# Token rows scattered to expert slots, results added in HBM, attention ahead of the routed experts

## The chip, the cores and the metric

One core of one Trainium2 chip runs the whole program. The metric is the device time of one execution in microseconds; the median of three runs stands for the kernel. A core has five engines that follow their own instruction streams and wait for one another by semaphores: PE (TensorE, matrix products, with its weight loads as PEld), DVE (VectorE), ACT (ScalarE), POOL (GpSimd) and SP (SyncE, which here only issues transfers). Indirect transfers, whose row numbers are data, are issued by POOL.

## The reference

2048 tokens of 128 numbers. With `xn` the layer norm of the input, the result is `x + attention(xn) + experts(xn)`.

```
xn = layernorm(x)
# attention, linear, 16 heads of 8
q, k, v = split(layer_norm(xn) @ Wqkv);  q, k = elu(q) + 1, elu(k) + 1
att = (q @ (k^T v)) / (q @ sum(k) + 1e-6)            # per head and batch
attention = xn + att @ Wout
# experts: 8, top 2, 640 slots each
top_v, top_i = top_k(xn @ Wg.T, 2);  gates = softmax(top_v)
pos  = running count of the expert's choices;  keep = pos < 640
h    = gelu(rows @ W1[:, :256]) * (rows @ W1[:, 256:]);  y = h @ W2
out[token] += gate * y[expert, slot]                 # for kept choices
```

## The kernel before

**Dense expert and routed experts.** Expert 0 is computed for all 2048 tokens in four groups of 512 and multiplied by a gate that is zero where it was not chosen. Experts 1 to 7 are routed: each has 640 slots, 5 tiles of 128 rows, computed as a step of 3 tiles and a step of 2 (`PARTS`). The first two dense groups run early, before attention's projections; the other two come last, after all routed steps (`DENSE_AFTER`). Products are made as three fp32r products of high and low halves (`product`, L973 to L975), so every input needs a split: the high half by ACT, the low half by a subtraction on POOL (`lower_w1`, L435, `xT_lo` L441) or DVE.

**Routing.** DVE takes the two best experts of each token (L749 to L760) from logits in a PSUM bank. PE counts the choices ahead of each (L1055, L1057), DVE turns the counts to slots (L772 to L784). Then a list of the token in each slot is made: DVE builds 0/1 matrices (`hot`, and `hot_row` of 128x4096 at L800), PE multiplies them (L1075, 32 matmuls), and DVE copies the list `slot_token` out (L817).

**Rows in and out.** `xn` is stored to HBM. POOL gathers the 35 tiles of 128 rows by 35 indirect transfers (`gather`, L459), five tiles per expert, and scatters the 35 result tiles by 35 indirect transfers (`scatter`, L471) into `y_rows`, which has one row per token and choice, zeroed before. Five experts' gathers are issued ahead of the first scatter (`GATHERS_AHEAD`), then the two take turns. In `y_rows` no two rows meet. At the end SP waits for all 35 scatters (L375), fetches both halves of `y_rows` in eight transfers (L378), DVE, ACT and POOL weight them by the gates and add them to the sum (L838, L663, L491), and SP stores the output (L385).

**Attention** is 14 pieces of work: four transposes of queries, and for eight pairs of tiles a numerator, a transpose and a projection. `ATT_FROM`, `ATT_EVERY` place them between the products of routed steps 9 to 14 and the dense ones after. The order of the work on each engine is written out by hand from these tables.

Of the kernel before, what the change touches and what calls it, by code (L numbers as in the profile page):

```python
# [5 lines left out]
F32 = mybir.dt.float32  # L20
# [17 lines left out]
DENSE_AFTER = (7, 7)  # L38
ATT_FROM = 36
ATT_EVERY = 2  # L40
ATT_DENSE = 14
GATHERS_AHEAD = 5
LO_EARLY = 2
EARLY_SUMS = 2
KV_LAG = 8
RESULTS_AT = 2
SLOTS_AT = 4
LIST_AT = 2
PRE_POOL = 2
DROPPED = 8192.0  # L50
PARTS = ((0, 3), (3, 2))


def moe_attention_block(nc, x, gamma, beta, wqkv, wout, wg_t, w1, w2, out):
# [15 lines left out]
    assert D == P and CAP % P == 0 and sum(n for _, n in PARTS) == ST and N <= 2048 and FC == 2  # L70

# [3 lines left out]
    steps = []  # L75
    for r, (e, j0, nj) in enumerate(routed_steps):
        steps.append((e, j0, nj, r))
        if (r + 1) % len(PARTS) == 0:
            steps += [step for step, after in zip(all_token_steps[EARLY:], DENSE_AFTER)
                      if after == (r + 1) // len(PARTS)]  # L80
    assert EARLY + len(steps) == len(routed_steps) + len(all_token_steps)
    S = len(steps)
    step_of_routed = [s for s in range(S) if steps[s][3] is not None]
    dense_steps = [s for s in range(S) if steps[s][3] is None]
    U = T // 2
    KT = TOP_K * T

# [7 lines left out]

    hurried = [s for s in range(1, S) if steps[s - 1][3] is not None and steps[s][3] is None][-1]
    spots = [(s, c, i) for s in range(S) for c in range(FC) for i in range(2)]
    chunks = [(s, c) for s in range(S) for c in range(FC)]
    pieces_at = {}
    i = ATT_FROM  # L100
    for piece in pieces:
        pieces_at.setdefault(spots[i] if i < len(spots) else "end", []).extend(piece)
        i += ATT_EVERY if i < 2 * FC * ATT_DENSE else 1

# [7 lines left out]
    for s, c in chunks:  # L112
        assert not pieces_at.get((s, c, 0)) or s >= EARLY_SUMS + EARLY
        if c == 0 and EARLY_SUMS <= s < EARLY_SUMS + EARLY:
            for j in range(GROUP):
                note_sum(("early", s - EARLY_SUMS), (all_token_steps[s - EARLY_SUMS][1] + j,))
        for kind, u in pieces_at.get((s, c, 0), []) + pieces_at.get((s, c, 1), []):
            if kind == "projection":
                note_sum((kind, u), (2 * u, 2 * u + 1))
        if s >= 1 and c == FC - 1 and steps[s - 1][3] is None:  # L120
            for j in range(GROUP):
                note_sum(("step", s - 1), (steps[s - 1][1] + j,))
    for kind, u in pieces_at.get("end", []):
        if kind == "projection":
            note_sum((kind, u), (2 * u, 2 * u + 1))
    assert steps[-1][1] == T - GROUP and steps[-1][3] is None
    for t in range(0, T, 2):
        if t == T - GROUP:
            for j in range(GROUP):
                note_sum(("step", S - 1), (t + j,))  # L130
        for k in range(TOP_K):
            note_sum(("fetched", t, k), (t,))
# [7 lines left out]
    xn_rows = nc.dram_tensor("xn_rows", [N, D], F32).ap()  # L140

    y_rows = nc.dram_tensor("y_rows", [TOP_K * N + R * CAP, D], F32).ap()
    xn_rows_tiles = xn_rows.rearrange("(t p) d -> p t d", p=P)
    y_rows_tiles = y_rows[0:TOP_K * N, :].rearrange("(t p) d -> p t d", p=P)

    with ExitStack() as ctx:
# [3 lines left out]
        def sem(name):  # L150
# [5 lines left out]
        xn = sb("xn", [P, T, D])  # L156
# [20 lines left out]
        iota_tiles = sb("iota_tiles", [P, RT, KT], F16)  # L177
        token_id = sb("token_id", [P, TOP_K, T], F16)
        first_slot = sb("first_slot", [P, T, E])
        rank = sb("rank", [P, T, E])  # L180
        eps = sb("eps", [P, 1])
        unused = sb("unused", [P, 1])
        unused_gelu = sb("unused_gelu", [P, 1])
# [10 lines left out]
        logit = sb("logit", [P, T, E])  # L194
# [4 lines left out]
        best = sb("best", [P, T])  # L199
# [3 lines left out]
        gate = [sb(f"gate{k}", [P, T]) for k in range(TOP_K)]  # L203
        gate_routed = [sb(f"gate_routed{k}", [P, T]) for k in range(TOP_K)]
        assigned = sb("assigned", [P, T, E], BF16)
        kept = sb("kept", [P, T, E])
# [5 lines left out]
        row_i = sb("row_i", [P, TOP_K, T], I32)  # L212
        tile_i = sb("tile_i", [P, TOP_K, T], I32)
        row_16 = sb("row_16", [P, TOP_K, T], F16)
        tile_16 = sb("tile_16", [P, TOP_K, T], F16)
        kept_routed = sb("kept_routed", [P, TOP_K, T])
        no_token = sb("no_token", [P, RT])
        vacant = sb("vacant", [P, RT])
        choices = sb("choices", [P, RT])
        target = sb("target", [P, RT])  # L220
        slot_target = sb("slot_target", [P, RT], I32)
        zeros = sb("zeros", [P, D])
        gate_dense = sb("gate_dense", [P, T, E])
        gate_part = sb("gate_part", [P, T, E])
        hot = sb("hot", [P, 2 * RT, KT], F16)
        hot_token, hot_tile = hot[:, 0:RT, :], hot[:, RT:2 * RT, :]
        slot_token = sb("slot_token", [P, RT], I32)

        gathered = sb("gathered", [P, RT, D])

        iota_rows = gathered[:, :, :].rearrange("p n d -> p (n d)")[:, 0:P * KT // 2] \
            .bitcast(F16).rearrange("p (r n) -> p r n", n=KT)
        xg_hi = [sb(f"xg_hi{i}", [P, 3 * P], F32R) for i in range(2)]
# [1007 lines left out]
```

## Time and profile before

| | |
|---|---|
| median of 3 runs | 187.8 us (181.33, 187.8, 189.93) |
| span of the profiled execution, first to last instruction | 156.1 us |
| median less span | 31.7 us |
| busiest engines | PE 111.6 us, POOL 99.3 us |

The profiled execution has only its span; its own device time is not given, so the difference to the median is what lies ahead of the first and behind the last instruction, together with the spread between runs. Busy shares are means over the span. A group of rows gives the idle time in front of its instructions and what ended it. The chain that ended last runs backwards from the last instruction through what released each wait; it tells which engine set the time in each stretch.

### The profile page before, as it was taken

To read this page: it belongs to the slowest core of one execution; us is meant where nothing else is said; L and a number is where in the kernel's file an instruction comes from. 1 tells how busy PE (TensorE), PEld (TensorE's weight loads), DVE (VectorE), ACT (ScalarE), POOL (GpSimd) and SP (SyncE) were. 2 spreads that over 40 slices of the span, in tenths; PEclk is the share of its full clock that TensorE was granted. 3 is DMA by queue.
4 is the path that set the end of the run, shared out by engine and by line. 5 is a ranking of instruction groups with operands and counts; after the bars stand their busy time and mean duration, and the time that the engine had idled before them with its cause. 6 is when DMAs were issued, how large, how long until landed. Compare 5 with 4: busy or idle time off the path is not lost.

```text
span 156.1 us, 2323 instructions
## 1 busy us (share of the span) xinstructions
PE 111.6 (72%) x745; PEld 103.8 (66%) x745; DVE 93.8 (60%) x251; ACT 72.2 (46%) x165; POOL 99.3 (64%) x111
## 2 busy tenths in 40 slices
PE   0029998399978996999999949609989999630000
PEld 0019975288978994999999949609989887620000
DVE  0699989999668838866535322504276565426940
ACT  0457669356659885054645535403243343124600
POOL 7950369934337777777777777777777777305540
PEclk9999999999999999599999999975899999996555
DMA  4999995000002222222121211121111111189540
GB/s 119 269 375 341 337 347 165 0 0 6 0 0 62 43 53 50 49 58 60 44 62 50 57 50 50 50 50 54 51 50 60 58 53 54 35 227 302 153 124 0
DMA packets 20827, 15.49 MB, mean 99 GB/s; under 512 B 2032, under 2 KB 18672, under 8 KB 20816
## 3 DMA queue, kind: packets, MB, share of 16 engines
q1 hardware_dynamic: 17856, 10.49, 22.7%
q0 software_dynamic: 2240, 4.59, 11.6%
q10 hardware_dynamic: 720, 0.27, 0.8%
q8 instruction: 6, 0.10, 0.3%
q14 instruction: 5, 0.04, 0.1%
HBM read 8.85 MB, written 6.49 MB: 98 GB/s over the span
## 4 chain that ended last, share of the span: by engine, by line
POOL 43%; DVE 16%; issue 15%; PE 11%; DMA 8%; ACT 2%; SPq 1%; DVEq 0%; POOLq 0%; ACTq 0%
POOL gathered L459 22%; POOL y_rows L471 21%; PE bank_y L993 4%; DVE xs L838 4%; DMA expo<-y_rows 4%; DMA xs<-in_x 3%; PE bank_a L1075 2%; PE bank_x L986 2%; DVE hid L765 2%; DMA y_rows<-gathered,slot_target 1%; DVE chosen L753 1%; PE bank_x L1046 1%; DVE stats L684 1%; DVE eq L751 1%; DVE xn L697 1%
## 5 line engine op out<-in xcount | busy, mean ns | idle before, releaser
L459 POOL DMA_INDIRECT gathered<-xn_rows,slot_token x35 | 34.3, 980 | 14.8 <-issue 10.4
L471 POOL DMA_INDIRECT y_rows<-gathered,slot_target x35 | 34.0, 972 | 10.7 <-issue 10.7
L940 DVE TENSOR_TENSOR hid<-gelu,bank_h 128x384 f32<-128x384 f32 (+2 forms) x32 | 16.4, 511 | 20.9 <-ACT gelu L645 20.5
L1197 PE MATMUL bank_y<-w_sb,hid 128*128 128x128 f32 x172 | 24.1, 293 | 1.3 <-issue 1.3
L1197 PEld LDWEIGHTS bank_y<-w_sb,hid 128*128 128x128 f32 x172 | 23.3, 210 | 1.5 <-issue 1.4
L645 ACT ACTIVATE gelu<-bank_h 128x384 f32<-128x384 f32 (+2 forms) x32 | 14.6, 458 | 19.8 <-PE bank_h L975 19.8
L973 PE MATMUL bank_h<-xg_hi,w_lo 128*128 128x384 f32 (+1 forms) x56 | 21.0, 375 | 1.3 <-DVE hid L940 0.9
L975 PE MATMUL bank_h<-xg_hi,w_hi 128*128 128x384 f32 (+1 forms) x56 | 17.8, 317 | 0.0
L974 PE MATMUL bank_h<-xg_lo,w_hi 128*128 128x384 f32 (+1 forms) x56 | 17.6, 315 | 0.0
L973 PEld LDWEIGHTS bank_h<-xg_hi,w_lo 128*128 128x128 f32 x56 | 11.1, 199 | 2.1 <-issue 1.3
L986 PE MATMUL bank_x<-ident,xn 128*128 128x128 f32 x16 | 4.4, 428 | 11.0 <-DVE xn L697 9.7
L491 POOL TENSOR_TENSOR xs<-xs,expo 128x256 f32<-128x256 f32 x8 | 6.1, 761 | 9.6 <-ACT expo L663 6.1
L1155 PE MATMUL bank_x<-ident,gathered 128*128 128x128 f32 x35 | 6.7, 292 | 7.6 <-DMA gathered<-xn_rows,slot_token 7.1
L628 ACT ACTIVATE gathered<-bank_y 128x384 f32<-128x384 f32 (+1 forms) x14 | 6.1, 438 | 12.5 <-PE bank_y L1197 12.5
L435 POOL TENSOR_TENSOR w_lo<-w_raw,w_hi 128x512 fp32r<-128x512 f32 x8 | 10.3, 1317 | 2.3 <-ACT w_hi L530 2.3
L913 DVE TENSOR_TENSOR xg_lo<-bank_x,xg_hi 128x384 fp32r<-128x384 f32 (+1 forms) x14 | 6.8, 488 | 8.1 <-ACT xg_hi L618 8.1
L838 DVE SCALAR_TENSOR_TENSOR xs<-expo,gate_routed,xs 128x128 f32<-128x128 f32 x16 | 8.0, 519 | 5.6 <-DMA expo<-y_rows 5.3
L974 PEld LDWEIGHTS bank_h<-xg_lo,w_hi 128*128 128x128 f32 x56 | 11.1, 198 | 0.0
L975 PEld LDWEIGHTS bank_h<-xg_hi,w_hi 128*128 128x128 f32 x56 | 11.0, 196 | 0.0
L986 PEld LDWEIGHTS bank_x<-ident,xn 128*128 128x128 f32 x16 | 3.2, 240 | 11.3 <-issue 9.6
L1155 PEld LDWEIGHTS bank_x<-ident,gathered 128*128 128x128 f32 x35 | 4.4, 147 | 8.8 <-DMA gathered<-xn_rows,slot_token 7.8
L618 ACT ACTIVATE xg_hi<-bank_x 128x384 fp32r<-128x384 f32 (+1 forms) x14 | 6.1, 436 | 8.3 <-PE bank_x L1155 8.3
(151 smaller groups left out, 266.8 us busy)
## 6 DMA issues: line engine op xcount, KB each, us to landing
w_raw<-in_w SPq DMA_DIRECT2D x4, 512.0 KB, 7.8
y_rows<-zeros SPq DMA_DIRECT2D x2, 1024.0 KB, 11.8
expo<-y_rows SPq DMA_DIRECT2D x8, 256.0 KB, 5.3
xs<-in_x SPq DMA_DIRECT2D x4, 256.0 KB, 4.6
xn_rows<-xn SPq DMA_DIRECT2D x4, 256.0 KB, 4.3
out_block<-xs SPq DMA_DIRECT2D x4, 256.0 KB, 2.3
w_sb<-in_w SPq DMA_DIRECT2D x1, 768.0 KB, 10.8
gathered<-xn_rows,slot_token POOLq DMA_INDIRECT x35, 2.7
```

What stands on the lines that cost most here:

```text
L435: nc.gpsimd.tensor_tensor(w1_lo[:, e, :], w1_raw[:, e, :], w1_hi[:, e, :].bitcast(F32), ALU.subtract).then_inc(w1_lo_ready, 1)
L459: nc.gpsimd.indirect_dma_start(gathered[:, n, :], None, xn_rows, bass.IndirectOffsetOnAxis(ap=slot_token[:, n:n + 1], axis=0),).then_inc(r ...
L471: nc.gpsimd.indirect_dma_start(y_rows, bass.IndirectOffsetOnAxis(ap=slot_target[:, n:n + 1], axis=0), gathered[:, n, :], None,).then_inc(y ...
L645: nc.scalar.activation(gelu[i % 2][:, 0:cols], bank_h[2 * c][:, 0:cols], ACT.Gelu).then_inc(gelu_ready, 1)
L838: nc.vector.scalar_tensor_tensor(acc[:, t, :], fetched[:, k, t, :], gate_routed[k][:, t:t + 1], acc[:, t, :], ALU.mult, ALU.add).then_inc( ...
L940: nc.vector.tensor_tensor(hid[s % 2][:, c, 0:cols], gelu[i % 2][:, 0:cols], bank_h[2 * c + 1][:, 0:cols], ALU.mult).then_inc(hid_ready, 1)
L973: nc.tensor.matmul(dst, a_lo, b_hi, start=True, stop=False)
L974: nc.tensor.matmul(dst, a_hi, b_lo, start=False, stop=False)
L975: return nc.tensor.matmul(dst, a_hi, b_hi, start=False, stop=True)
L986: ins = nc.tensor.transpose(bank_x[g % 2][:, j * P:(j + 1) * P], xn[:, g * GROUP + j, :], ident[:, :])
L1155: ins = nc.tensor.transpose(bank_x[0][:, j * P:(j + 1) * P], gathered[:, n, :], ident[:, :])
L1197: ins = nc.tensor.matmul(bank_y[:, j * D:(j + 1) * D], hid[s % 2][:, c, j * P:(j + 1) * P], w2_sb[:, e, c, :], start=(c == 0), stop=(c == ...
```

## The change

The routed rows go the other way round. Each row of `xa` holds the 128 numbers of `xn`, the token's number, its two expert ranks and its two gates (136 numbers). POOL scatters the 16 token tiles twice, once per choice, straight to the experts' slots in HBM; choices of expert 0 and dropped ones have a slot out of bounds and are skipped. The slots were filled with vacant rows, whose token numbers point behind the real ones. SP then reads each expert's 640 slots back in one plain transfer. The list of slots, its 0/1 matrices and its 48 matmuls are gone. ACT multiplies the results by the slot's gate as it leaves PSUM (one instruction per tile), and POOL adds them to one of two zeroed sums in HBM, even and odd experts apart, waiting before each expert for the additions of the expert two before. The fetched sums need one addition per group and side.

The two late dense groups and all attention now come before the routed steps; the 14 pieces lie in the first six places between products. The low halves of most weights move from POOL to DVE, ELU is written with one ACT instruction less, and two activation tables are loaded earlier.

```diff
-    steps = []
-    for r, (e, j0, nj) in enumerate(routed_steps):
-        steps.append((e, j0, nj, r))
...
+    steps = all_token_steps[EARLY:] + [(e, j0, nj, r) for r, (e, j0, nj) in enumerate(routed_steps)]
...
+    for i, piece in enumerate(pieces):
+        pieces_at.setdefault(spots[i * PIECE_SPOTS // len(pieces)], []).extend(piece)
...
@@ sync
+            for r in range(R):
+                sp.dma_start(x_slots_tiles[:, r, :, :], vacant[:, :, :]).then_inc(vacant_stored, 16)
...
+            sp.wait_ge(rows_out, 16 * TOP_K * T)
+            for r in range(R):
+                sp.dma_start(rows[:, r * ST:(r + 1) * ST, :], x_slots_tiles[:, r, :, :]).then_inc(rows_in[r], 16)
+            for i in (1, 0):
+                sp.wait_ge(y_added[i], 16 * ST * len(range(i, R, 2)))
+                for g in range(G):
+                    sp.dma_start(fetched[:, i, g * GROUP:(g + 1) * GROUP, :],
+                                 y_sums_tiles[i][:, g * GROUP:(g + 1) * GROUP, :]).then_inc(fetched_in[i][g], 16)
...
@@ gpsimd
-            def gather(r):
-                for n in range(r * ST, (r + 1) * ST):
-                    nc.gpsimd.indirect_dma_start(
-                        gathered[:, n, :], None, xn_rows,
-                        bass.IndirectOffsetOnAxis(ap=slot_token[:, n:n + 1], axis=0),
-                    ).then_inc(rows_in[r], 16)
...
+            pool.wait_ge(vacant_stored, 16 * R)
+            pool.wait_ge(xn_act_ready, G)
+            for k in range(TOP_K):
+                pool.wait_ge(slots_ready, k + 1)
+                for t in range(T):
+                    nc.gpsimd.indirect_dma_start(
+                        x_slots, bass.IndirectOffsetOnAxis(ap=slot_i[:, k, t:t + 1], axis=0), xa[:, t, :], None,
+                        bounds_check=R * CAP - 1, oob_is_err=False,
+                    ).then_inc(rows_out, 16)
+            pool.wait_ge(zeros_stored, 16 * 2)
+            for r in range(R):
+                if r >= 2:
+                    pool.wait_ge(y_added[r % 2], 16 * ST * (r // 2))
                 for i, (j0, nj) in enumerate(PARTS):
                     pool.wait_ge(y_evac, len(PARTS) * r + i + 1)
                     for n in range(r * ST + j0, r * ST + j0 + nj):
                         nc.gpsimd.indirect_dma_start(
-                            y_rows, bass.IndirectOffsetOnAxis(ap=slot_target[:, n:n + 1], axis=0),
-                            gathered[:, n, :], None,
-                        ).then_inc(y_stored, 16)
+                            y_sums[r % 2],
+                            bass.IndirectOffsetOnAxis(ap=rows[:, n, TOKEN:TOKEN + 1].bitcast(I32), axis=0),
+                            rows[:, n, 0:D], None, compute_op=ALU.add,
+                        ).then_inc(y_added[r % 2], 16)
...
@@ vector
+            for k in range(TOP_K):
+                link(nc.vector.tensor_tensor(picked[:, k, :, :], chosen[:, k, :, :], slot_all[:, :, :], ALU.mult))
+                link(nc.vector.tensor_reduce(slot[:, k, :], picked[:, k, :, :], AX.X, ALU.add))
+                nc.vector.tensor_copy(slot_i[:, k, :], slot[:, k, :]).then_inc(slots_ready, 1)
...
+            def add_fetched(side, g):
+                group = slice(g * GROUP, (g + 1) * GROUP)
+                dve.wait_ge(fetched_in[side][g], 16)
+                before_sum(tuple(range(g * GROUP, (g + 1) * GROUP)))
+                nc.vector.tensor_tensor(acc[:, group, :], acc[:, group, :], fetched[:, side, group, :],
+                                        ALU.add).then_inc(acc_added, 1)
```

The order on POOL, from the low halves to the end of the program; first before, where the gathers (`gathered<-xn_rows`) and the scatters (`y_rows<-gathered`) take turns:

```order
L441 TENSOR_TENSOR xT_lo<-pre,xT_hi 128x512
L435 TENSOR_TENSOR w_lo<-w_raw,w_hi 128x512 x7
L451 TENSOR_TENSOR pre<-pre,bias 128x256 x2
L459 DMA gathered<-xn_rows,slot_token 128x128 x25
L471 DMA y_rows<-gathered,slot_target 8576x128 x5
L459 DMA gathered<-xn_rows,slot_token 128x128 x5
L471 DMA y_rows<-gathered,slot_target 8576x128 x5
L459 DMA gathered<-xn_rows,slot_token 128x128 x5
L471 DMA y_rows<-gathered,slot_target 8576x128 x25
L491 TENSOR_TENSOR xs<-xs,expo 128x2x128 x8
```

and after the change:

```order
L374 MEMSET head_cols 128x16
L375 AFFINE_SELECT head_cols<-head_cols 128x16
L377 AFFINE_SELECT head_cols<-head_cols 128x16
L379 COPY head_block<-head_cols 128x128
L383 TENSOR_TENSOR w_lo<-w_raw,w_hi 128x512
L386 TENSOR_TENSOR xT_lo<-pre,xT_hi 128x512
L395 DMA x_slots<-xa,slot_i 4480x136 x32
L408 DMA y_sums<-rows 2688x128 x35
L111 UNCONDITIONAL_BRANCH
```

The 70 indirect transfers are 67; all 32 of the first kind now stand ahead of all 35 of the second, and the sums behind them are gone from POOL.

The order on SP, from the second weight load on (`x_slots<-vacant` fills the slots, `rows<-x_slots` reads them back); after the change:

```order
L310 DMA x_slots<-vacant 128x5x136 x7
L302 DMA w_raw<-in_w 128x2x512 x3
L313 DMA w_sb<-in_w 128x12x128
L318 DMA y_sums<-zeros 128x21x128 x2
L324 DMA rows<-x_slots 128x5x136 x7
L330 DMA expo<-y_sums 128x4x128 x8
L334 DMA out_block<-xs 128x4x128 x4
```

Seven transfers of vacant rows now stand ahead of three weight loads, and seven that read the slots back stand where nothing stood; the four stores of `xn` are gone.

## Rows read from the trace of the kernel before

**Rows 1.** The page: span, busy time, traffic by slice, and the chain that ended last.

```profile
span 156.1 us, 2323 instructions
PE 111.6 (72%) x745; PEld 103.8 (66%) x745; DVE 93.8 (60%) x251; ACT 72.2 (46%) x165; POOL 99.3 (64%) x111
...
GB/s 119 269 375 341 337 347 165 0 0 6 0 0 62 43 53 50 49 58 60 44 62 50 57 50 50 50 50 54 51 50 60 58 53 54 35 227 302 153 124 0
...
POOL 43%; DVE 16%; issue 15%; PE 11%; DMA 8%; ACT 2%; SPq 1%; DVEq 0%; POOLq 0%; ACTq 0%
```

**Rows 2.** Groups by line, POOL: busy us, mean ns, idle before, releaser.

```profile
L459 POOL DMA_INDIRECT gathered<-xn_rows,slot_token x35 | 34.3, 980 | 14.8 <-issue 10.4 <-DVE slot_token L817 4.4
L471 POOL DMA_INDIRECT y_rows<-gathered,slot_target x35 | 34.0, 972 | 10.7 <-issue 10.7
```

**Rows 3.** The tile gathered: ns min/median/max and starts; us to landing.

```profile
L459 POOL DMA_INDIRECT gathered<-xn_rows,slot_token x35: 940/944/1449, 45.0 to 101.5; - x35
...
DMA to landing us min/median/max: 2.2/2.5/4.0
```

**Rows 4.** The chain that ended last, 20 to 46 us: start, us, what.

```profile
21.38 0.30 DVE top L749
...
27.55 1.24 DVE assigned L758
...
39.99 3.89 PE bank_a L1075 x32
43.91 0.21 DVE slot_token L817
...
44.97 1.14 POOL gathered L459
```

**Rows 5.** Timeline of DVE in the routing: start, us, engine, line, what.

```profile
22.03 0.30 DVE L751 TENSOR_TENSOR eq<-eq,rank 128x128 f32<-128x128 f32 x1
...
24.97 1.26 DVE L751 TENSOR_TENSOR eq<-eq,rank 128x128 f32<-128x128 f32 x1
```

**Rows 6.** Timeline of POOL in the same stretch.

```profile
23.45 8.96 POOL L435 TENSOR_TENSOR w_lo<-w_raw,w_hi 128x512 fp32r<-128x512 f32 x7
```

**Rows 7.** Timeline of ACT: the table load in the first normalisation.

```profile
6.18 1.28 ACT L505 ACT_TABLE_LOAD   x1 [6.18 <-DVE mv L687]
```

**Rows 8.** Timeline of PE: last eight tiles of attention's input projections.

```profile
47.05 0.41 PE L973 MATMUL bank_h<-wqkv_hi,xT_lo 128*128 128x384 f32 x1 [1.06 <-ACT val L568]
...
53.80 1.15 PE L1099 MATMUL bank_a<-hot,qT 128*128 128x35 f16 x16
```

**Rows 9.** Timeline of PE: one routed expert's first product to the next's.

```profile
72.56 0.42 PE L973 MATMUL bank_h<-xg_hi,w_lo 128*128 128x384 f32 x1
...
77.59 1.50 PE L1197 MATMUL bank_y<-w_sb,hid 128*128 128x128 f32 x12
78.84 0.42 PE L973 MATMUL bank_h<-xg_hi,w_lo 128*128 128x384 f32 x1
```

**Rows 10.** Timeline of PE where it waited for gathered rows, and after.

```profile
91.94 0.55 PE L1155 MATMUL bank_x<-ident,gathered 128*128 128x128 f32 x3 [2.23 <-DMA gathered<-xn_rows,slot_token]
...
105.09 0.90 PE L1155 MATMUL bank_x<-ident,gathered 128*128 128x128 f32 x3 [4.85 <-DMA gathered<-xn_rows,slot_token]
...
108.46 2.49 PE L1197 MATMUL bank_y<-w_sb,hid 128*128 128x128 f32 x12
```

**Rows 11.** Timeline of DVE: one pair of tiles of attention, first and last instruction.

```profile
126.29 0.18 DVE L846 TENSOR_SCALAR den<-bank_a 128x32 f32<-128x32 f32 x1
...
126.89 0.42 DVE L850 TENSOR_TENSOR att<-bank_a,den_inv 128x256 f32<-128x256 f32 x1
```

**Rows 12.** The chain that ended last: the last scatter, issue and landing.

```profile
133.36 2.24 DMA y_rows<-gathered,slot_target
```

**Rows 13.** Timeline of DVE, 134 us to the end: first and last weighted sums.

```profile
139.48 1.77 DVE L838 SCALAR_TENSOR_TENSOR xs<-expo,gate_routed,xs 128x128 f32<-128x128 f32 x4 [3.83 <-DMA expo<-y_rows]
...
148.10 2.06 DVE L838 SCALAR_TENSOR_TENSOR xs<-expo,gate_routed,xs 128x128 f32<-128x128 f32 x4
```

More of the change, by code:

```diff
@@ L110, in note_sum @@
         sums_with[name] = len(sum_tiles)
[L112 to L120, printed above, removed]
+    for i in range(EARLY):
+        for j in range(GROUP):
+            note_sum(("early", i), (all_token_steps[i][1] + j,))
+    for s in range(S):
+        for c in range(FC):
+            for i in range(2):
+                for kind, u in pieces_at.get((s, c, i), []):
+                    if kind == "projection":
+                        note_sum((kind, u), (2 * u, 2 * u + 1))
+        if s >= 1 and steps[s - 1][3] is None:
             for j in range(GROUP):
                 note_sum(("step", s - 1), (steps[s - 1][1] + j,))
[L123 to L132, printed above, removed]
+    for side in (1, 0):
+        for g in range(G):
+            note_sum(("routed", side, g), tuple(range(g * GROUP, (g + 1) * GROUP)))
     def earlier_sum(index, tiles):
@@ L139, in moe_attention_block @@
     out_tiles = out.rearrange("b (t p) d -> p (b t) d", p=P)
[L140 to L144, printed above, removed]
+    x_slots = nc.dram_tensor("x_slots", [R * CAP, ROW], F32).ap()
+    x_slots_tiles = x_slots.rearrange("(r j p) w -> p r j w", p=P, j=ST)
+    y_sums = [nc.dram_tensor(f"y_sums{i}", [N + CAP, D], F32).ap() for i in range(2)]
+    y_sums_tiles = [y.rearrange("(t p) d -> p t d", p=P) for y in y_sums]
     with ExitStack() as ctx:
@@ L211, in moe_attention_block @@
         slot_i = sb("slot_i", [P, TOP_K, T], I32)
[L212 to L232, printed above, removed]
+        gate_dense = sb("gate_dense", [P, T])
+        gate_part = sb("gate_part", [P, T])
+        gate_pair = sb("gate_pair", [P, RT, TOP_K])
+        gate_slot = sb("gate_slot", [P, RT])
+        rows = sb("rows", [P, RT, ROW])
         xg_hi = [sb(f"xg_hi{i}", [P, 3 * P], F32R) for i in range(2)]
@@ L543, in _ @@
             transposed(2)
+            upper_w1(0)
             act.wait_ge(var2_ready, 1)
@@ L1089, in kv_tile @@
                     ins.then_inc(kv_added, 1)
[L1091 removed]
+            for t in range(T):
+                if t == RESULTS_AT:
+                    early_results(1)
                 qkv_tile(t)
[L1093 to L1101 removed]
+                if t >= KV_LAG:
+                    kv_tile(t - KV_LAG)
+            for t in range(T - KV_LAG, T):
+                kv_tile(t)
             bank_x0_read = [(early_y, EARLY)]
@@ L1199, in down @@
                 ins.then_inc(down_done, 1)
-            transpose_slots(0)
-            for t in range(T - KV_LAG, T):
-                kv_tile(t)
             pe.wait_ge(val_ready, T)
@@ L1206, in _ @@
                 up(s)
-                if s >= 1 and s != hurried:
+                if s >= 1:
                     down(s - 1)
             down(S - 1)
-            for piece in pieces_at.get("end", []):
-                attention_piece(*piece)
 def kernel(L0_attn_x, L0_attn_gamma, L0_attn_beta, L0_attn_Wqkv, L0_attn_Wout, L0_ffn_Wg, L0_ffn_W1, L0_ffn_W2):
```

483 lines of the change are left out of this document (172 added, 311 removed).

## The prediction

> **What bounds the kernel now.** I read the page first: the span is 156.1 us, and neither PE nor POOL is busy for more than three quarters of it; yet the chain that ended last runs 43% on POOL, and most of its "issue" is the pause between POOL's transfers [rows 1]. The groups by line show why: 35 gathers of 0.98 us and 35 scatters of 0.97 us, each after a pause of some 0.30 us (10.4 and 10.7 us in all), so 1.25 to 1.27 us a tile [rows 2]. From the first gather at 44.97 [rows 4] to the last scatter at 133.36 [rows 12] POOL does nothing else. Three other stretches count. Until 44.97 the routing and the making of the slot list hold everything: DVE from 21.38 to 28.79, then slots, 0/1 matrices, 3.9 us of PE and the copy of the list at 43.91 [rows 4]. PE follows POOL: a routed expert takes 78.84 − 72.56 = 6.28 us of unbroken PE work [rows 9], five gathers 6.25, and PE waits 2.23 and 4.85 us once gathers stand behind scatters [rows 10]. Behind the last scatter come 22.7 us of tail: landing 2.24, fetch, weighted sums of DVE from 139.48 to 150.16, output [rows 12, 13].
>
> **The start.** The first table load of 1.28 us stands in the first normalisation [rows 7]; loaded earlier it is hidden. DVE has other work around it, so I take 1.2 us: logits at 20.2 in place of 21.4. The routing chain of 12 instructions lasts 7.4 us. The same instruction takes 0.30 us at 22.03 and 1.26 at 24.97 [rows 5], when POOL has begun its seven low halves [rows 6]; these leave POOL, so I take 12 times 0.33, which is 4.0, and 0.3 for the gap, now in the chain: choices at 24.5. But PE counts only behind the first dense products, which end 1.2 us earlier than before, near 25.5, and takes 0.7: counts at 26.2. Six instructions of 0.3 give the first choice's slots at 28.1. From the list to the first gather was 44.97 − 44.12 = 0.85 us [rows 4]; so the first scatter starts at **29.0**, 16 us earlier. 2.4 MB of vacant rows stand ahead on SP, 4.2 MB in all before they are down; at the 300 GB/s and more of slices 3 to 6 [rows 1] that is near 15 us, and hides. The three weight loads behind them slip by 8 us, to near 23, but their halves are now made after 38. The zeroes end near 31, needed after 85.
>
> **32 scatters of 544-byte rows.** The trace has no row of this width and no skipped slot. Nearest is the scatter of 512-byte rows, 0.972 us and 0.305 of pause [rows 2]; a gather at its fastest is 0.94, at its slowest 1.449 [rows 3]. I take the scatter's own, 32 × 1.277 = 40.9; the ends are −1 us (32 × 0.03) and +15.3 us (32 × 0.477).
> Beside DVE's dense stretch transfers stretch: the median gather is 0.944, the mean 0.980, so 35 gathers lost 1.3 us, nearly all while attention's projections ran [rows 2, 3]. All 32 now lie beside such work; I add 2.0 us, with 0 and 9 as ends.
> The Trainium skill ("SBUF — State Buffer", section "Who interferes with whom") says that a DVE instruction with two SBUF inputs and a GpSimd one that reads SBUF exclude each other for a whole instruction. Read so, the 14 or so of DVE here would cost up to 9 us in place of 2; the trace's gathers, mostly at 0.94 beside the same instructions, speak against it.
> Together 29.0 + 40.9 + 2.0 = 71.9. Landing was 2.5 us in the median [rows 3]: 74.4. Then SP reads back the first expert, 348 KB. DVE waited 3.83 us for the first 512 KB of the fetch [rows 13]; I take 3.2: rows at **77.6**.
>
> **Does PE fill the time?** Removed are 48 small matmuls of 3.9 and 1.15 us [rows 4, 8]. Projections start near 34.4, 1.4 us earlier; eight tiles take 53.80 − 47.05 = 6.75 us [rows 8], 16 take 13.5, with 1.6 for early results: 49.5. States 2 us. In attention a pair costs DVE 1.02 us from 126.29 to 127.31 [rows 11]; with PE's numerator and transpose and the handing over it is 2.0, eight pairs 16, and some 6 for queries, early sums and the weight halves between: **74**. So PE waits some 3.5 us for rows. Before, a wait of 4.85 us left it slower: 12 matmuls took 2.49 in place of 1.50 us [rows 9, 10]. At that ratio some 4 us of work would cost 2.5 more; after 3.5 us of waiting I leave it out of the sum and keep it for the range.
>
> **To the first addition.** Twelve result matmuls take 78.84 − 77.59 = 1.25 us, 0.104 each; an expert's 20 take 2.1 of its 6.28 us, and 4.2 are left for products with their transposes, 2.5 for three tiles and 1.7 for two [rows 9]. Ahead of the first addition stand half a dense group of four tiles (1.7), 16 result matmuls for each of two dense groups (3.3), the first expert's products (4.2) and first 12 results (1.25), and by my estimate 0.9 for ACT's evacuation and 0.4 for the hand-over: 11.8 us, **89.4**. ACT's five small evacuations per expert, for two before, stay beside PE's work.
>
> **35 additions.** The trace has no adding transfer. I take the scatter's price again: 35 × 1.277 = 44.7, just above PE's 7 × 6.28 = 44.0, so POOL runs through to **134.1**. Ends: −1.2 us (35 × 0.033, the fastest gather) and +16.7 us (35 × 0.477, the slowest). The new wait for the expert two before is 6.4 us old when it is reached and lands in 2.5 [rows 3]: nothing.
>
> **The tail.** The last scatter began at 133.36, the last addition begins at 132.8: for all the rebuilding, POOL is free no sooner. The gain is behind it. Landing 2.5 (135.3), issue and first group 3.3, three more groups of 256 KB 0.9 each: 141.3. One addition of four tiles 0.7: 142.0. No gates, no ACT, no POOL, and the odd side lies ahead. Before, DVE ended at 150.16 [rows 13], 5.9 us before the end of the span; 142.0 + 5.9 = **148.0**. That is 8.1 us less. All of this is against the profiled span of 156.1; the median of 187.8 is 31.7 more, which I leave as it is: **179.7 us**.
>
> **Rivals.**
> (a) An adding transfer is dearer than a storing one. At 1.449 us each the sum grows by 16.7: 196.4, slower. It eats the gain from 0.23 us each (8.1 / 35), and is slower by 2% from 0.34. For it: it reads HBM as well as SBUF, and the waits of every second expert turn real once landing passes 6.4 us. Against: queue 0 moves 64 KB per tile where far more was moved per us at the start [rows 1]. The end could be further out if descriptors are made twice. Chance 0.25.
> The Trainium skill ("DMA: Bandwidth & Descriptors", section "SWDGE vs HWDGE vs iDMA") gives one read and one write descriptor per copy, and "Collectives: The Full Stack" ("The bandwidth ceiling") two reads for an add, with half the rate. Three descriptors for two would make 0.97 into 1.46 us; it is this rival, and no row here shows it.
> (b) The first 32 scatters are dearer, by their width, by the bounds or by DVE. PE stands idle behind them, so all goes to the end: +7 to +9 gives 187 to 189. Chance 0.12.
> (c) PE is the late one: attention's pairs at 2.6 us in place of 2.0 bring it to 79, and with PE slow after the wait the end is 4 later: 184. Chance 0.08.
> (d) Scatters at a gather's price and a shorter way to the first addition: 174 to 176. Chance 0.05.
> (e) The early start fails: the vacant rows, in 544-byte pieces, are down only after 29 us. They would have to move at under 100 GB/s. Within (b).
>
> **Numbers.** Forecast 0.50, its own range 174 to 185. What a measurement can tell from no change is 2%, 184.0 to 191.6. Faster: nearly all of the forecast, (d) and half of (c), 0.54; same: most of (b), rests of (c) and the forecast, 0.20; slower: (a) and a little of (b), 0.26. The range of 172 to 197 leaves out the far end of (a).
>
> **What would show it.** Right: first scatter to `x_slots` at 29, last near 71; PE waits 2 to 5 us for `rows`; 35 additions one after another at 1.28; first one near 89; the last fetch's sums under 1 us a group. Wrong: an addition whose mean is over 1.2 us or with idle time that landing ends; a first scatter later than 32; PE reaching the first expert's transposes after its rows; or a median that leaves the span by other than 32 us.

## The result, and the profile after

The changed kernel takes 206.6 us (median of 4 runs, 206.3 to 207.2), the kernel before beside it 188.9 (4 runs, 181.3 to 193.4): 1.142 times as long, 95% interval 1.136 to 1.148. The prediction was 179.7 with a range of 172 to 197 and faster as its likeliest side; it was wrong in both.

The profiled execution of the kernel before (span 156.1 us), on which the prediction rests, is free of a disturbance that its timed runs of this set and those of the change had. It is told below as "the hold", and the comparison is made on a chip without it too. On which chips this first set ran, and the profile of before, is not on record.

The page of the changed kernel, its span, engines, queue 0 and groups of instructions (busy us, mean ns, idle before, releaser):

```profile
span 204.7 us, 2254 instructions
PE 111.1 (54%) x697; PEld 100.0 (49%) x697; DVE 87.7 (43%) x255; ACT 69.8 (34%) x164; POOL 93.5 (46%) x90
...
q0 software_dynamic: 6064, 4.26, 15.6%
...
L408 POOL DMA_INDIRECT y_sums<-rows x35 | 54.7, 1562 | 68.2 <-ACT rows L539 58.8
L395 POOL DMA_INDIRECT x_slots<-xa,slot_i x32 | 31.9, 998 | 20.5 <-DVE kept L673 11.1
...
L707 DVE SCALAR_TENSOR_TENSOR pre<-bank_h,inv,bias 128x256 f32<-128x256 f32 x16 | 7.7, 483 | 39.0 <-remote 30.5
```

Against [rows 2]: the 32 scatters of token rows cost what a scatter cost before, 1.00 us for 0.97; the 35 additions cost 1.56. POOL waits 58.8 us for results, 57.9 of them for the first expert's. The last row shows why: DVE waited 30.5 us for results of PE's projections. "Remote" means that no instruction in the trace ended when the semaphore rose. This is the timeline of DVE in that stretch, with the idle time before an instruction in brackets:

```profile
39.51 0.48 DVE L707 SCALAR_TENSOR_TENSOR pre<-bank_h,inv,bias 128x256 f32<-128x256 f32 x1 [2.67 <-PE bank_h L851]
40.83 0.48 DVE L707 SCALAR_TENSOR_TENSOR pre<-bank_h,inv,bias 128x256 f32<-128x256 f32 x1 [0.84 <-PE bank_h L851]
53.52 0.48 DVE L707 SCALAR_TENSOR_TENSOR pre<-bank_h,inv,bias 128x256 f32<-128x256 f32 x1 [12.20 <-remote]
57.74 0.48 DVE L707 SCALAR_TENSOR_TENSOR pre<-bank_h,inv,bias 128x256 f32<-128x256 f32 x1 [3.74 <-remote]
...
64.78 0.48 DVE L707 SCALAR_TENSOR_TENSOR pre<-bank_h,inv,bias 128x256 f32<-128x256 f32 x1 [5.95 <-remote]
73.88 0.48 DVE L707 SCALAR_TENSOR_TENSOR pre<-bank_h,inv,bias 128x256 f32<-128x256 f32 x1 [8.62 <-remote]
```

And PE, which made the tiles that DVE takes at 53.52, 57.74 and 64.78:

```profile
40.36 0.34 PE L851 MATMUL bank_h<-wqkv_hi,xT_hi 128*128 128x384 f32 x1
...
40.90 0.34 PE L851 MATMUL bank_h<-wqkv_hi,xT_hi 128*128 128x384 f32 x1
...
42.90 0.34 PE L851 MATMUL bank_h<-wqkv_hi,xT_hi 128*128 128x384 f32 x1
```

Their last products start by 42.90, and DVE goes on 12.8, 16.5 and 21.5 us after the ends that the trace models, that is, when their semaphores rise. In the run without scatters (e18, below) this takes 0.1 us: a product that ends at 36.58 is taken at 36.70. POOL's scatters go on at their pace of 1.28 us all the while. This is **the hold**: from 37 to 74 us PE's results come out late, the next tiles find no free buffer, and everything behind slips.

Is it PE's clock? These are the windows of the same run (us; busy us of PE, PEld, DVE, ACT, POOL; granted clock; DMA share; GB/s):

```profile
40.00:44.00 4.00, 2.00 (x11) 1.38 (x9) 0.48 (x1) 1.24 (x3) 3.05 (x4) 1.00 0.14 47
44.00:48.00 4.00, 0.00 (x0) 0.00 (x0) 0.00 (x0) 0.00 (x0) 3.08 (x4) 0.68 0.15 51
48.00:54.00 6.00, 0.00 (x0) 0.00 (x0) 0.48 (x1) 0.00 (x0) 4.57 (x5) 0.50 0.15 50
```

The three late products were made at a granted clock of 1.00 (2.4 GHz); it falls to 0.50 (1.2 GHz) only after PE has stood idle. The low clock follows the hold and does not cause it.

### The profile page after: what moved, and what is told of

Same layout as the page of the kernel before. It is cut to its first block, busy times and chain, and to the rows that moved or that the text cites. A ratio compares the mean times of both kernels' runs of the same rounds, so it can differ in the third digit from the quotient of the medians.

```text
span 204.7 us, 2254 instructions
## 1 busy us (share of the span) xinstructions
PE 111.1 (54%) x697; PEld 100.0 (49%) x697; DVE 87.7 (43%) x255; ACT 69.8 (34%) x164; POOL 93.5 (46%) x90
## 3 DMA queue, kind: packets, MB, share of 16 engines
q0 software_dynamic: 6064, 4.26, 15.6%
## 4 chain that ended last, share of the span: by engine, by line
PE 48%; another core or an unknown queue 15%; DVE 13%; POOL 9%; DMA 6%; issue 3%; ACT 3%; POOLq 1%; SPq 0%; ACTq 0%
PE bank_y L1057 9%; POOL y_sums L408 9%; PE bank_h L849 8%; PE bank_h L851 7%; PE bank_h L850 7%; PE bank_y L869 3%; DMA expo<-y_sums 2%; DVE pre L707 2%; PE bank_x L1016 2%; PE bank_y L949 2%; DMA xs<-in_x 2%; DVE pre L713 2%; PE bank_x L920 2%; DMA y_sums<-rows 2%
## 5 line engine op out<-in xcount | busy, mean ns | idle before, releaser
L408 POOL DMA_INDIRECT y_sums<-rows x35 | 54.7, 1562 | 68.2 <-ACT rows L539 58.8
L395 POOL DMA_INDIRECT x_slots<-xa,slot_i x32 | 31.9, 998 | 20.5 <-DVE kept L673 11.1
L949 PE MATMUL bank_y<-val,pre 128*128 128x130 f32 x32 | 8.1, 352 | 31.1 <-issue 15.7
L707 DVE SCALAR_TENSOR_TENSOR pre<-bank_h,inv,bias 128x256 f32<-128x256 f32 x16 | 7.7, 483 | 39.0 <-remote 30.5
L949 PEld LDWEIGHTS bank_y<-val,pre 128*128 128x128 f32 x32 | 6.4, 235 | 33.5 <-DVE pre L713 17.5
L738 DVE TENSOR_TENSOR xs<-xs,expo 128x512 f32<-128x512 f32 x8 | 5.5, 692 | 32.6 <-DMA expo<-y_sums 32.2
L500 ACT ACTIVATE expo<-pre,minus_one 128x512 f32<-128x512 f32 x8 | 5.8, 722 | 37.5 <-DVE pre L707 34.8
L539 ACT ACTIVATE rows<-bank_y,gate_slot 128x128 f32<-128x128 f32 x35 | 10.6, 365 | 11.2 <-PE bank_y L1057 11.2
L849 PE MATMUL bank_h<-xT_hi,w_lo 128*128 128x512 f32 x16 | 9.3, 581 | 3.8 <-DVE hid L689 3.8
L849 PE MATMUL bank_h<-wqkv_hi,xT_lo 128*128 128x384 f32 x16 | 7.8, 487 | 1.2 <-issue 1.2
```

Source lines behind the costliest of these rows:

```text
L395: nc.gpsimd.indirect_dma_start(x_slots, bass.IndirectOffsetOnAxis(ap=slot_i[:, k, t:t + 1], axis=0), xa[:, t, :], None, bounds_check=R * C ...
L408: nc.gpsimd.indirect_dma_start(y_sums[r % 2], bass.IndirectOffsetOnAxis(ap=rows[:, n, TOKEN:TOKEN + 1].bitcast(I32), axis=0), rows[:, n, 0 ...
L539: ins = nc.scalar.activation(rows[:, n, 0:D], bank_y[:, j * D:(j + 1) * D], ACT.Copy, scale=gate_slot[:, n:n + 1])
L707: nc.vector.scalar_tensor_tensor(pre[:, t, :], bank_h[t % 4][:, 0:2 * D], inv2[:, t:t + 1], bias[:, 0:2 * D], ALU.mult, ALU.add).then_inc( ...
L849: nc.tensor.matmul(dst, a_lo, b_hi, start=True, stop=False)
L949: ins = nc.tensor.matmul(bank_y[:, b * (D + 2):(b + 1) * (D + 2)], pre[:, t, D:2 * D], val[:, t, :], start=(t % TB == 0), stop=(t % TB == ...
```

## The experiments

Two chips (6 and 7) show the hold; there the kernel before takes 190 to 191 us. Two others (5 and 11) do not; there it takes 157 to 159. "Held" and "not held" below name the kind. Each ratio is to the kernel before on the same chip. The changed kernel as it stands was run on one of these four, chip 5 (e9).

**First set, held** (kernel before 191.4 us). What is it in the scatters that costs?

```
e1:  slots of dropped rows clamped to spare rows of x_slots; no bounds test
e2:  xa[:, t, 0:D] in place of xa[:, t, :]     (512-byte rows, no metadata)
e3:  the 35 additions without compute_op=ALU.add
e4:  the kernel before, its 35 scatters with compute_op=ALU.add
```

> The changed kernel with its 32 scatters of token rows all in range: a choice that has no routed slot goes to a spare row of its own behind the slots, and the bounds test is gone (one small DVE operation takes the place of a copy). In the changed kernel the matmuls of attention's projections end up to 21 us after they were issued, from 37 to 74 us, and the first routed product begins at 119. Theory A (skipped, out of range rows disturb the core): the stall of 31 us goes, attention is done near 80 and PE reaches the routed rows some 35 us earlier; time near 172 us. Theory B (rows of 544 bytes) and theory C (any scatter beside projections does it): unchanged, 205 to 208 us.

Measured 204.9 us, ratio 1.071 (1.062 to 1.080), POOL idle 57.8 us before the additions: skipped rows are not the cause of the hold.

> The changed kernel with scatters of 512 bytes in place of 544: token numbers, ranks and gates are left out of the rows and set beforehand (numbers of rows behind the tokens, gates of zero), so the routed experts' share is missing from the output; the bounds test and the skipped rows stay. Theory B (the width): the stall from 37 to 74 us goes, time near 172 us. Theory A (skipped rows) and theory C (any scatter beside projections): unchanged within 2 us, 203 to 208 us.

Measured 204.3 us, ratio 1.067 (1.058 to 1.076): nor is the width.

> The changed kernel with its 35 adding transfers turned to storing ones (where two experts' rows meet in a sum, one is lost). An adding one took 1.542 us and a pause of 0.30, a storing one of before 0.97 and the same pause. If the adding itself is what costs, each falls to 0.97; PE's pace of 6.28 us per expert and POOL's 6.35 then almost meet, 35 x 0.57 = 20 us go: near 187 us. If rows whose indices lie in strided columns, or the wider source, are the price, it stays at 1.54 and 206 us.

Measured 195.9 us (193.6 to 198.1), ratio 1.012 (1.003 to 1.021). With the same indices and the same source POOL's stores take 0.97 us again, so the adding itself is what costs. The hold is still there, and the time falls only by some 10 us against e1 and e2 beside it, where 20 were expected: even the lowest of its four times is 6.6 us over the 187. In the profiled execution (197.3 us) PE was busy in 8.6 to 8.8 of each 10 us while stores ran (130 to 160 us), against 10.0 while additions did.

> The kernel before with its 35 scatters of results turned to adding ones and nothing else (each target row is zero before, and hit once). POOL is its bound from 45 to 134 us, so the price shows whole: if adding costs 0.57 us, 35 x 0.57 = 20 us more, a ratio near 1.10. If adding is free and the changed kernel's 1.54 us has another reason, ratio 1.00.

Measured 192.8 us, ratio 1.007 (1.001 to 1.013), where 1.10 was expected. Its additions take 1.56 us each as well, 20.7 us of work more than in the profile of before, and the end moves by 1.4. Here POOL stands idle for 13.0 us behind the held PE before its first addition (90.9 us) and then works on without a gap until its last one at 167.1. So in the kernel before on this chip, whose stores cost less, POOL must have stood idle for most of the 20 us behind PE. That is argued from the sum: there is no trace of the kernel before on a held chip.

**Second set, not held** (157.9 us). Here the hold was to be located, and was absent, so none of these four tells of it.

```
e5:  the kernel before, unchanged
e6:  the 32 scatters left out; SP's wait for them too
e7:  pool.wait_ge(rows_out[0], 16 * n)   ahead of scatter n
e8:  pool.wait_ge(kv_added, B)           ahead of the first scatter
```

> The kernel before, unchanged, to have a second profiled execution of it. Theory C (indirect transfers of POOL beside PE's projections hold PE's results back, in nearly all executions and not in the one that the prediction rested on): the span is 186 to 191 us, the projections' semaphores are raised 10 to 20 us behind their last matmul between 56 and 80 us, and what is left between the time and the span is about 2 us. Rival (the 31.7 us lie outside the span): the span is 155 to 158 us again.

Span 155.6, time 157.4 us: the span of the rival, but what is outside is 1.8 us, not 31.7. In every run that has both numbers 1.7 to 2.1 us lie outside the span.

> The changed kernel without its 32 scatters of token rows (POOL only waits for the slots; the experts' slots stay vacant, so the routed experts compute on zero rows and add them to the spare rows; the additions all stay). Theory C: with no indirect transfer beside them the projections end near 50 us and attention near 75; the rows, read back early, do not hold PE, the first addition comes near 87 and 35 additions of 1.84 us end near 152; with 11 us of tail 163 to 168 us. Rival D (the stall comes from PE's own work or its place, not from the transfers): PE is held from 37 to 74 us as before and the time stays at 203 to 207 us.

175.6 us, no late semaphore, where 163 to 168 were expected. The row below shows what remains:

```profile
L403 POOL DMA_INDIRECT y_sums<-rows x35: 1545/1545/2031, 98.1 to 161.2; - x35
```

The first addition comes at 98.1 and not at 87, with no scatters at all, so it is PE that is late.

> The changed kernel, each of the 32 scatters waiting until the one before has landed, 3.2 to 3.7 us apart in place of 1.28, so rows are complete near 29 + 32 x 3.5 = 141 us. If the stall needs transfers close together (theory C1), it is gone: projections end near 50 us, attention near 75, and PE then waits for rows until about 145; first addition near 157, end near 225 to 235 us. If a transfer costs PE the same however far apart (C2), PE's results are late throughout 37 to 141 us, though none of it would show in the end, since rows are later still.

227.0 us, as expected; scatters 3.3 us apart in the mean, first addition at 151.0, six us before the expected 157.

> The changed kernel, the first scatter held until both attention states are summed. Projections then run with no indirect transfer beside them and end near 50 us (both theories but D). The 32 scatters lie beside attention and the dense group, from 52 to 93 us. If the stall follows the transfers (C), PE's results are late by 10 us and more from about 60 to 93 us, attention ends near 112, first addition near 125 and the time is about 203 us. If only the projections' kind of work is held (C3), attention ends near 76, PE waits for rows until about 99, first addition near 111, and the time is 188 to 191 us.

196.2 us, between the two expectations: no late semaphore, first addition 117.6. Between scatters that end at 98 and the first addition lie 20 us. On this chip it tells of the order alone: delayed to 56 us, the scatters do reach the end.

**Third set, not held** (157.2 us).

> The changed kernel, unchanged, beside the kernel before on one chip. The kernel before has now given 157 to 158 us in one set of runs (no projection semaphore late) and 189 to 191 us in others (late by up to 21 us). If this set is of the first kind: rows are complete near 75, but PE comes to them near 84 as in the run without scatters; first addition 98, 35 additions at 1.85 us to 163, time 176 to 179 us, ratio 1.11 to 1.14. If it is of the second: 205 to 207 us against 188 to 192, ratio 1.07 to 1.10.

174.1 us (4 runs, 173.0 to 174.4), 2 us under the range, ratio 1.104 (1.094 to 1.113), span 172.4. This is the run to set against the prediction. Its tiles x_slots and y_sums (ns min/median/max, first and last start):

```profile
L395 POOL DMA_INDIRECT x_slots<-xa,slot_i x32: 966/972/1485, 28.4 to 69.9; - x32
...
L324 SPq DMA_DIRECT2D rows<-x_slots x7: 359/533/2117, 72.2 to 76.1; - x7
```

```profile
L408 POOL DMA_INDIRECT y_sums<-rows x35: 1541/1541/1819, 96.4 to 159.2; - x35
```

The edit of e6, run twice more on this chip, took 175.2 us (e10) and 173.7 us (e16, with e13 to e15): with nothing held, taking all 32 scatters away saves nothing. In e16 the first addition starts at 96.5, as here; PE alone sets it.

> The changed kernel, each of the 32 scatters waiting until the second one before it has landed: 1.7 to 2.0 us apart in place of 1.28, as the additions are. Rows complete near 29 + 32 x 1.85 + 2.5 = 91 us. Where the stall is present and theory C1 (transfers close together) holds: no late semaphore, PE waits for rows until 94, first addition near 107, time 184 to 188 us, 20 us less than the changed kernel beside it. C2 (any spacing): PE is late as before, 203 to 210 us. In a set without the stall: first addition near 107 in place of 98, 8 to 10 us more than the changed kernel beside it.

179.8 us (2 runs), 5.7 more than the changed kernel beside it, where I expected 8 to 10: scatters 27.9 to 81.6, first addition 101.6. Whether this pace would keep PE from being held is open; it was not run on a held chip.

> The changed kernel with two edits: results are stored, not added, into one row for each token and choice (target row = token + 2048 for the second choice, worked out by DVE with two small instructions for each expert; a vacant slot's store is skipped), and the attention pieces lie between the products of the first seven steps in place of the first one and a half, so PE starts the routed experts at 75 to 80 us. Sum: first store near 92, then whichever is longer, 35 x 1.28 = 45 us or PE's 44 us with some 12 us of attention in it: last store 140 to 148, fetch of both halves 10 us, output 6: 154 to 164 us without the stall, ratio to before 0.98 to 1.04. If the additions' price is not what costs (rival), it stays over 170 us. With the stall present: 30 us more.

The main lines, shortened:

```
 y_rows = nc.dram_tensor("y_rows", [TOP_K * N, D], F32)
 second = (rows[.., RANKS + 1] is_equal E - e) mult N
 target = second + rows[.., TOKEN]
 indirect_dma_start(y_rows, target[:, n], rows[:, n, 0:D], bounds_check=TOP_K * N - 1)
 PIECE_SPOTS = 28                    # places for the 14 attention pieces; 6 in the change
```

166.0 us, ratio 1.054 (1.047 to 1.061): 8 us less than the change, 2 over my range. POOL's stores have gaps until 118 us, for PE now does attention between the experts.

**Fourth set, not held** (159.0 us): the additions' price taken away (e13), the late start attacked (e14), then both (e15).

> The changed kernel with results stored, not added, into one row for each token and choice; attention stays where the change put it. Theory F (35 transfers in a row set the end, at the price of an adding one): first store at 96.4 as before it, 34 steps of 1.28 in place of 1.85 us, so the last begins at 140; both halves are fetched behind it, 15.7 us to the end as in the run with spread attention: span 155.8, time 157 to 159 us where the kernel before takes 157, 16 us less than the changed kernel. Rival G (PE's experts set the end, the additions only fill the time): 7 experts of 6.3 us from 96 end near 140 in any case, and stores gain under 5 us over the additions: 169 us and more. With the projections held: 31 us more.

157.7 us (10 runs), ratio 0.993 (0.989 to 0.997), span 156.1. Theory F holds to a third of a microsecond, and G, under which the stores would have gained less than 5 us, has fallen: the additions' price is worth 16 us to the end. Even so this kernel is within 2% of the kernel before, and no clear gain. The row that answers to the additions:

```profile
L413 POOL DMA_INDIRECT y_rows<-rows,target x35 | 34.2, 978 | 35.2 <-ACT rows L544 25.2 <-issue 10.1
```

> The changed kernel with its additions, its attention pieces spread over the first three steps in place of the first one and a half (one number): part of attention now lies behind the first expert's products. PE would reach the rows at 76 to 78 in place of 82.5 and be done with the first results at 91 to 93. If the start is worth its full size (F): span 172.4 - 4 = 167 to 169, time 169 to 171 us. If spread pieces cost PE as much behind the rows as they save ahead of them (H): first addition at 95 to 97 and 173 to 175 us. With the projections held: 31 us more.

177.7 us (2 runs). Neither: worse than H, with the first addition at 100.2. PE's timeline has the reason:

```profile
75.59 0.90 PE L1016 MATMUL bank_x<-ident,rows 128*128 128x128 f32 x3 [6.81 <-DMA rows<-x_slots]
```

PE now comes to the rows 6.8 us before they are there, waits, and has the rest of attention still to do behind them. The order in which the change has it, attention first, uses that time.

> Both: results stored into a row for each token and choice, attention pieces over the first three steps. F: first store at 91 to 93, the last at 135 to 137, span 151 to 153, time 153 to 155 us, ratio to the kernel before 0.97 to 0.99. H: as with the stores alone, 157 to 159. With the projections held: 31 us more.

161.6 us, ratio 1.020 (1.011 to 1.029): 3.9 more than stores alone, the same loss again. F was wrong on the order and right on the price. No run brings PE sooner to its work on the rows without putting attention behind them, so the late start's share in the time is read from the trace and not shown by an edit.

**Fifth set, held** (190.1 us).

> The run with stores alone, and of the two dense steps ahead of the routed experts one moved behind the last of them; all attention pieces lie between the first two products of the dense step that is left. From PE's first rows to the first store it was 96.4 - 83.7 = 12.7 us; one step's second half of products (1.7) and its 16 results (1.7) leave that stretch, and half of its products leave the stretch of attention, which is held by latency. If PE's late start sets the first store (theory F), it comes 3 to 5 us earlier, at 91.5 to 93.5, the last at 135 to 137, the span is 151 to 153 and the time 153 to 155, ratio to the kernel before 0.965 to 0.985. Rival: pieces in two lumps, without products between them, make PE slower (its clock falls, pairs over 2.06 us), and the first store stays at 95 to 97: 157 us, ratio 0.99 to 1.0. With the projections held: 31 us more.

192.9 to 204.6 us over 4 runs, median 200.8, too scattered for a verdict. The hold is there (three of DVE's waits, each of 8 to 10 us, end with "remote", at 46.3, 61.1 and 72.3), first store at 128.2, and stores come in groups with pauses behind PE, as in e3. Whether one dense step behind the experts helps an undisturbed chip is open.

> The changed kernel without its 32 scatters of token rows, once more, for a set in which projections are held: theory C 174 to 177 us and no late semaphore before the first addition, rival D about 205 us with projections late from 37 to 74. In a set without the hold: 174 us, and the question stays open.

173.7 us (2 runs, 172.4 and 175.0), ratio 0.916 (0.905 to 0.928), where the kernel before takes 190.1 and the change, in the first set, 206.6. It leaves out work, so the ratio is no gain. With e17, which has the scatters and the hold on the same chip, it is the pair that settles the hold. Timeline of DVE from 36 us, without the scatters:

```profile
36.70 0.93 DVE L702 SCALAR_TENSOR_TENSOR pre<-bank_h,inv,bias 128x256 f32<-128x256 f32 x2 [1.28 <-PE bank_h L846]
39.46 1.02 DVE L702 SCALAR_TENSOR_TENSOR pre<-bank_h,inv,bias 128x256 f32<-128x256 f32 x2 [1.82 <-PE bank_h L846]
...
40.99 0.48 DVE L702 SCALAR_TENSOR_TENSOR pre<-bank_h,inv,bias 128x256 f32<-128x256 f32 x1
42.20 0.48 DVE L702 SCALAR_TENSOR_TENSOR pre<-bank_h,inv,bias 128x256 f32<-128x256 f32 x1 [0.73 <-PE bank_h L846]
```

One tile every 1.1 us and no "remote" row, where the change had pauses of 4 to 12 us. On these chips PE is held while POOL's indirect transfers run 1.28 us apart; take them away and it is not. Theory C stands, rival D has fallen. The time is that of e16 on the chip that is not held, 173.7 us. By what path one engine's transfers delay another's results the records don't show.

## Why the prediction was wrong, point by point

The undisturbed run (e9, span 172.4) is set against the predicted span of 148.0. The parts of the difference of 24.4 us:

- **First scatter**, predicted 29.0: 28.4 there and 29.0 in the result's own trace. Right.
- **32 scatters**, predicted 1.277 us apart and 2.0 us for DVE beside them: the last starts at 69.9, the first rows are fetched from 72.2 and there at 75, predicted 77.6. Right, with 2.6 us to spare. Their sum of 33.0 us is 1.9 over 32 × 0.972, close to the 2.0 that I took from the trace. In the held run, where DVE mostly stands idle, the sum is 31.9 us, and only the two scatters at 29 to 32 us are long. The Trainium skill ("SBUF — State Buffer", "Who interferes with whom") gave up to 9 by my reading, that each of DVE's two-input instructions shuts POOL's transfer out; the trace disagrees with that reading. The section itself says that a `tensor_tensor` did not stall a DMA, and infers that making descriptors needs the write side of the shared ports, where a `tensor_tensor` takes only the read side.
- **Does PE fill the time?** Here the first term failed. PE was to come free at 74; its first `rows` transposes stand at 82.45, where nothing waits for a transfer any more:

```profile
81.17 0.68 PE L1003 MATMUL bank_x<-wout_sb,attT 128*128 128x128 f32 x4 [1.34 <-DVE xs L757]
82.45 0.88 PE L1016 MATMUL bank_x<-ident,rows 128*128 128x128 f32 x3 [0.60 <-DVE xs L757]
```

  Projections end at 53.1 for 49.5, 3.6 us late. From there my terms were 2 for states, 16 for pairs, 6 for the rest. Measured: states 3.3 to 56.4, queries and the first pair's start 6.5, the pairs' seven steps 15.3, and 3.6 from the last pair's division to the end of its output projection: 28.7. The pair itself was right; its two starts in DVE's timeline are 2.06 us apart for 2.0:

```profile
62.90 0.42 DVE L750 TENSOR_TENSOR att<-bank_a,den_inv 128x256 f32<-128x256 f32 x1
...
64.96 0.42 DVE L750 TENSOR_TENSOR att<-bank_a,den_inv 128x256 f32<-128x256 f32 x1
```

  What failed is what stood around it, above all the lead and the run-out of a chain that goes PE, DVE, PE, ACT, PE: 4.7 us on top of the 3.6. This is rival (c) in its effect, later still than its 79, and not in its cause, which was a pair of 2.6 us.
- **From rows to first addition**: 96.41 − 82.45 = 14.0 us, predicted 11.8 (89.4 − 77.6). Half a dense step took 2.5 us (82.98 to 85.49) for 1.7. PE came to it after a stretch with gaps (busy 1.5 of 3.4 us, 79.0 to 82.4) and had a granted clock of 0.53 from 82.4 to 85.4. In the held run, at 1.00, the same half step takes 1.5 us (115.88 to 117.35), and the way from `rows` to the first addition 12.7 us, so the clock is some 1.3 of the 2.2. The prediction had seen this term and left it out of its sum. With the late PE the first addition is 7.0 us late.
- **35 additions**, predicted 1.277 us apart: 1.848. From the first start to the last 62.8 us for 43.4, so 19.4 us. This is rival (a), in kind right and dearer than its end of 1.449 + 0.30; I gave it 0.25. The sum took the price of a storing scatter for an adding one because no row had one, and I named against it that queue 0 had bandwidth to spare. It has, and that decided nothing. Queue 0 counts 6064 packets: 32 scatters at 32, and 35 additions at 144 (the run without scatters has 5040). An addition puts 4.5 times the packets on its queue. Whether the packets are what takes POOL's time the runs do not show.
- **The tail**: from the start of the last addition to the end of the span 172.4 − 159.2 = 13.2 us, predicted 148.0 − 132.8 = 15.2. Right in kind, 2.0 us better.

So 7.0 + 19.4 − 2.0 = 24.4 us. The step that failed is **"I take the scatter's price again: 35 × 1.277"**, with the **74** at which PE was to come free behind it. e13 confirms the first by itself: same first start (96.42), 34 steps in 43.6 us for 62.8, and 2.9 us more of tail for a second half to fetch, together 16.3 us of span less. For the second no edit does the same; what shows it is that PE is as late without any scatters (e6, e10, e16).

The Trainium skill ("Collectives: The Full Stack", "The bandwidth ceiling", with "DMA: Bandwidth & Descriptors", "SWDGE vs HWDGE vs iDMA") gave, by my estimate, three descriptors for two, so 1.46 us. The trace has 1.54. That came far nearer than the 0.97 that I took; that no row showed it was a reason to test it, not to price it at nothing. The packets, 144 for 32, do not stand as three for two, so the near hit may be luck.

**"31.7 more, which I leave as it is"** was right in its size by luck. The text ahead of the prediction put the difference down to what lies outside the span and to the spread between runs; outside the span lie 2 us. The rest is the hold, 190 against 157 for the kernel before, and the change has it as well: 206.6 against 174.1 is 32.5. Both kernels run a burst of POOL's indirect transfers 1.25 to 1.28 us apart beside PE's work: 25 gathers beside the last projections and the first expert before, 32 scatters beside projections and attention now. A change without such a burst there would have been free of the hold, as e18 is, and gained some 33 us by it on these chips; the sum would have missed that too. A profiled execution 31.7 us under the median was another kind of execution than the timed ones; that should have been a rival with a chance of its own. The forecast of 179.7 was 26.9 us too low: 24.4 in the span and 2.5 here (206.6 less the undisturbed span of 172.4 is 34.2, for 31.7).

## What to carry to other kernels

Price an indirect transfer that adds as another instruction: 1.54 us for 128 rows of 512 bytes where one that stores takes 0.97. As a rule of thumb from this case, it pays only if what it saves elsewhere (here a second fetch, 3 us) exceeds 0.57 us a tile, and a row of one's own for each contribution, summed at the end, is the cheaper way when POOL is the bound. When work is taken off a critical engine, write out the other engine's whole chain up to the point where the two meet: the scatters were ready at 75, and PE was not there until 82. And when a profiled execution is far from the median, find out what differs before any sum is carried from one to the other; here 1.7 to 2.1 us would have been the whole of what lies outside the span.

## What the runs showed of the hardware

- An adding indirect transfer: 1.54 to 1.57 us in the mean of each of 13 runs, 144 packets on queue 0 for 128 rows; a storing one 0.97 and 32 packets.
- Skipped rows (e1) and 544-byte rows in place of 512 (e2) do not change a scatter's price: 1.00 us in the mean with and without them (changed kernel, e1, e2).
- Single scatters and gathers take up to 1.5 us in place of 0.97 or 0.94. In the change the first two of the burst do, 1.49 and 1.28 us, but this is no price of a burst's start: in e7 they are those at 28.7 (1.48) and 49.4 (1.44), in the profile of before those at 52.7 (1.45) and 54.4 (1.25). The cause is open.
- The hold: PE's results up to 21.5 us late on two chips of four, with the kernel before 32 us slower there. It starts 9 to 11 us after the first indirect transfer (transfers from 29.0 and the first product over 1 us late at 37.9 in the change, 46.0 and 57.2 in e4), ends 4 to 5 us after the burst's last transfer has begun (69.4 and 73.9, 76.9 and 81.9), and is absent without the transfers. Additions 1.85 us apart do not bring it; stores 1.28 apart do, in a milder form. This is how PE's busy time shows it, in windows of 10 us (PE, PEld, DVE, ACT, POOL, granted clock, DMA share, GB/s), first e3 on a held chip:

```profile
130.00:140.00 10.00, 8.63 (x68) 8.12 (x67) 4.21 (x11) 5.06 (x15) 6.04 (x7) 1.00 0.12 41
140.00:150.00 10.00, 8.58 (x67) 8.06 (x66) 5.06 (x14) 4.70 (x14) 5.76 (x6) 1.00 0.12 40
```

then e13, with stores at the same pace, on one that is not held:

```profile
110.00:120.00 10.00, 10.00 (x82) 9.97 (x81) 5.59 (x18) 5.90 (x18) 7.56 (x9) 1.00 0.15 49
120.00:130.00 10.00, 10.00 (x77) 9.92 (x77) 4.68 (x13) 6.59 (x19) 7.56 (x9) 1.00 0.11 34
```

  and the changed kernel, with additions, on a held chip:

```profile
130.00:140.00 10.00, 10.00 (x80) 9.96 (x80) 5.75 (x15) 6.37 (x19) 8.35 (x6) 1.00 0.42 36
140.00:150.00 10.00, 10.00 (x80) 9.93 (x79) 4.55 (x12) 6.54 (x19) 8.48 (x6) 1.00 0.43 39
```

  The granted clock is 1.00 in all six, so the clock is not the reason. Open are the path, and whether the spacing alone decides, since no paced scatter ran on a held chip.
